# Third head in PSUM, two powers as one operation, GpSimd's additions side by side, and DVE's top keys in front of the turn of the expert weights

## The reference, cut to what matters

```
n1  = layernorm(x)
q, k, v = n1 @ Wq.T, n1 @ Wk.T, n1 @ Wv.T ; sq, sk = elu(q) + 1, elu(k) + 1
memory_part = (sq @ memory) / clip(sq @ memory_norm)
local_part  = causal linear attention(sq, sk, v), in chunks of 128, with a state S += sk.T @ v per chunk
x_mid = x + layernorm((g * memory_part + (1 - g) * local_part) @ Wo.T)

n2  = layernorm(x_mid)
dense   = silu(n2 @ Wup.T) @ Wdown.T                          # inner size 1024
routing: 4 heads, each with 64 + 64 key scores; top 8 of both sides, the 8 best of their sums
w       = silu((n2 . down_embed[i]) * softmax(best sums))     # for the 8 chosen of 1024 experts, per head
experts = sum of w * up_embed[i] over heads and choices
out = x_mid + layernorm(dense + experts)
```

## Time and profile before

| what | value |
|---|---|
| median of 3 runs | 2870.93 us (2860.86 to 2872.65) |
| profiled execution | 2865.48 us, its span 2863.7 us |
| PE (TensorE) busy | 2790.7 us, 97% |
| DVE busy | 2550.8 us, 89% |
| ACT (ScalarE) busy | 2547.9 us, 89% |
| POOL (GpSimd) busy | 2320.0 us, 81% |
| chain that ended last | POOL 50%, DVE 26%, issue 10%, PE 7%, ACT 5% |
| granted TensorE clock | 0.998 |

### The profile page before, as it was taken

The page is one execution under the profiler, slowest core; times in us unless marked ns, Lnnn a source line. Parts: engine busy times, 40 slices in busy tenths (PEclk is TensorE's granted clock), DMA queues, the critical chain, the costliest instruction groups (busy, mean ns, idle before and its releaser), DMA issues.

```text
span 2863.7 us, 46938 instructions
## 1 busy us (share of the span) xinstructions
PE 2790.7 (97%) x13306; PEld 2178.3 (76%) x13306; DVE 2550.8 (89%) x6346; ACT 2547.9 (89%) x3692; POOL 2320.0 (81%) x2556
## 2 busy tenths in 40 slices
PE   8999999999999999999999999999999999999998
PEld 7677777777777777777777777777777777777776
DVE  6898899999998899999999999999999899998886
ACT  6888988899889898998898989988999899899997
POOL 5767788788888888888888888888888888888884
PEclk9999999999999999999999999999999999999999
DMA  4787887788878887888788778877887788788764
GB/s 134 152 165 161 175 169 165 159 173 173 169 158 175 162 174 158 171 174 170 158 178 170 164 164 173 169 165 166 173 174 161 168 173 173 162 175 170 146 155 114
DMA packets 609031, 471.50 MB, mean 165 GB/s; under 512 B 362371, under 2 KB 543492, under 8 KB 608772
## 3 DMA queue, kind: packets, MB, share of 16 engines
q0 software_dynamic: 52832, 199.77, 39.5%
q1 hardware_dynamic: 555940, 268.74, 38.2%
HBM read 137.37 MB, written 131.20 MB: 94 GB/s over the span
## 4 chain that ended last, share of the span: by engine, by line
POOL 50%; DVE 26%; issue 10%; PE 7%; ACT 5%; DMA 0%; DVEq 0%; POOLq 0%; ACTq 0%
POOL sums L678 21%; POOL rstd L626 13%; PE banks L854 6%; POOL wexp L753 5%; DVE prob_odd L1426 4%; DVE w_blocks L1460 4%; POOL h_diff L657 3%; POOL cand_best L736 2%; DVE x_mid L1551 2%; POOL cdif L756 2%; DVE sums L1384 2%; ACT wexp L1152 2%; POOL hT L670 2%; ACT wexp L1155 2%; DVE picked L1388 2%
## 5 line engine op out<-in xcount | busy, mean ns | idle before, releaser
L678 POOL TENSOR_TENSOR sums<-scores 128x1024 f32<-128x1024 f32 x512 | 1022.2, 2111 | 70.4 <-ACT scores L1286 63.1
L626 POOL TENSOR_TENSOR rstd<-var_eps,minus_half 128x1 f32<-128x1 f32 x512 | 554.8, 1164 | 46.1 <-ACT y_sq L1141 21.0
L854 PE MATMUL banks<-deT,xn2T 128*128 128x512 f32 x1024 | 482.5, 594 | 2.6 <-DVE picked L1388 2.2
L854 PE MATMUL banks<-xn2T,wupT 128*128 128x256 f32 (+1 forms) x2272 | 465.4, 359 | 3.2 <-DVE state L1519 2.5
L854 PE MATMUL banks<-ue,gT 128*128 128x256 f32 x2048 | 464.5, 380 | 3.0 <-ACT gT L1216 3.0
L854 PEld LDWEIGHTS banks<-ue,gT 128*128 128x128 f32 x2048 | 390.0, 191 | 56.6 <-ACT gT L1216 3.4
L854 PEld LDWEIGHTS banks<-xn2T,wupT 128*128 128x128 f32 x2272 | 390.1, 191 | 46.5 <-DVE state L1519 3.3
L854 PEld LDWEIGHTS banks<-deT,xn2T 128*128 128x128 f32 x1024 | 185.3, 191 | 135.1 <-issue 124.4
L1152 ACT ACTIVATE wexp<-prob_odd 128x1024 f32<-128x1024 f32 x127 | 134.4, 1059 | 134.0 <-DVE w_blocks L1460 133.8
L854 PE MATMUL banks<-route,xn2T 128*128 128x512 f32 x512 | 240.8, 592 | 0.8 <-ACT xn2T L1116 0.8
L854 PE MATMUL banks<-wdownT,hT 128*128 128x128 f32 (+1 forms) x1608 | 239.3, 294 | 0.1
(11 more groups left out here) (190 smaller groups left out, 7272.7 us busy)
## 6 DMA issues: line engine op xcount, KB each, us to landing
wexp<-wexp POOLq DMA_DIRECT2D x127, 1024.0 KB, 10.4
wexp<-wexp POOLq DMA_DIRECT2D x127, 512.0 KB, 5.2
w_way<-w_blocks SPq DMA_DIRECT2D x127, 512.0 KB, 3.1
g_parts<-w_way SPq DMA_DIRECT2D x508, 128.0 KB, 7.6
xn_way<-xn_blocks SPq DMA_DIRECT2D x992, 32.0 KB, 1.7
x_in<-_attn_hidden_states_dram SPq DMA_DIRECT2D x128, 128.0 KB, 6.0
out_dram<-x_out SPq DMA_DIRECT2D x128, 128.0 KB, 4.6
xn1T<-xn_way SPq DMA_DIRECT2D x125, 128.0 KB, 3.9
```

Source lines behind the costliest of these rows:

```text
L626: return nc.gpsimd.tensor_tensor(rstd[:, n, m:m + 1], var_eps[:, n, m:m + 1], minus_half[:, :], ALU.pow)
L678: return nc.gpsimd.tensor_tensor(sums[:, k, :, :], scores[:, k, 0:XIN].unsqueeze(2).broadcast_to([P, XIN, NKEYS]), scores[:, HEADS + k, :] ...
L854: last = nc.tensor.matmul(out, lhs(c), rhs(c), start=(start and c == 0), stop=(stop and c == chunks - 1), skip_group_check=shared)
```

## The change

TOPS = TILES makes the first of two places for the top keys the only one: ahead of the turn L1460. GpSimd's body is put in another order, and two powers are one operation where a step has both. Head 2's pick is written over `down` in PSUM, in place of `picked[:, 0, :]`. TensorE then waits for head 2's weighing.

```diff
-    TOPS = 3
+    TOPS = TILES
...
+        def with_y(k):
+
+            found = [u for u in (k - 7, k - 6) if u >= 0 and seven(u) == (k - u == 7)]
+            return found[0] if len(found) == 1 else None
...
+            def two_powers(a, b):
+                cols = slice(a, b + 1, b - a)
+                r, v = (x[:, :, :].rearrange("p n m -> p (n m)")[:, cols] for x in (rstd, var_eps))
+                return nc.gpsimd.tensor_tensor(r, v, minus_half[:, :].broadcast_to([P, 2]), ALU.pow)
...
             def body(t, steady):
+                if t[7] is not None:
+                    pool.wait_ge(s_mix_var_eps, t[7] + 1)
+                    if with_y(t[7]) is None:
+                        power(LN_O, t[7] % 2).then_inc(s_mix_rstd, 1)
+                    else:
+                        pool.wait_ge(s_y_var_eps, with_y(t[7]) + 1)
+                        two_powers(2 * LN_O + t[7] % 2, 2 * LN_Y + with_y(t[7]) % 2).then_inc(s_mix_rstd, 1)
                 if t[9] is not None:
                     key_sums(3).then_inc(s_head_3_sums_ready, 1)
-                if t[7] is not None:
-                    pool.wait_ge(s_mix_var_eps, t[7] + 1)
-                    power(LN_O, t[7] % 2).then_inc(s_mix_rstd, 1)
...
+                for y in ([t[14]] if seven(t[14]) else []) + ([t[13]] if plain(t[13]) else []):
+                    if t[7] is None or with_y(t[7]) is None:
+                        pool.wait_ge(s_y_var_eps, y + 1)
+                        power(LN_Y, y % 2).then_inc(s_y_rstd, 1)
+                if t[7] is not None:
+                    pool.wait_ge(s_x_mid_var_eps, t[7] + 1)
+                    power(LN_M, t[7] % 2).then_inc(s_x_mid_rstd, 1)
                 if seven(t[11]) and t[11] % 2 == 0:
                     h_difference(t[11])
                 if seven(t[12]) and t[12] % 2 == 0:
                     h_three(t[12])
-                if seven(t[14]):
-                    pool.wait_ge(s_y_var_eps, t[14] + 1)
-                    power(LN_Y, t[14] % 2).then_inc(s_y_rstd, 1)
-                if plain(t[13]):
-                    pool.wait_ge(s_y_var_eps, t[13] + 1)
-                    power(LN_Y, t[13] % 2).then_inc(s_y_rstd, 1)
-                if t[7] is not None:
-                    pool.wait_ge(s_x_mid_var_eps, t[7] + 1)
-                    power(LN_M, t[7] % 2).then_inc(s_x_mid_rstd, 1)
...
                 if seven(t[11]):
-                    pool.wait_ge(s_head_3_weighed, t[9] + 1)
                     if t[11] % 2 == 0:
                         h_second_row(t[11])
...
                 if t[9] is not None:
                     if t[9] == 0:
                         pe.wait_ge(s_set_sb, SET_DOWN)
-                    if not steady:
-                        wait(pe, s_head_2_selected, t[9])
+                    wait(pe, s_head_2_weighed, t[9])
                     product(d_ps[0], DC, lambda c: xn2T[:, c, t[9] % TURNED, :], lambda c: deT[:, c, 0:HALF]).then_inc(s_down_0_in_psum, 1)
...
                     dve.wait_ge(s_head_2_sums_ready, t[10] + 1)
-                    dve.wait_ge(s_head_0_weighed, t[10] + 1)
-                    nc.vector.scalar_tensor_tensor(picked[:, 0, :], head(sums, 2), best[:, 2, TOP - 1:TOP], down,
+                    nc.vector.scalar_tensor_tensor(down, head(sums, 2), best[:, 2, TOP - 1:TOP], down,
                                                    ALU.is_ge, ALU.mult).then_inc(s_head_2_selected, 1)
...
-                    nc.vector.scalar_tensor_tensor(prob[2], picked[:, 0, :], rz[:, t[10] % 2, 2:3], prob[2],
+                    nc.vector.scalar_tensor_tensor(prob[2], down, rz[:, t[10] % 2, 2:3], prob[2],
                                                    ALU.mult, ALU.mult).then_inc(s_head_2_weighed, 1)
```

More of the change, by code:

```diff
@@ L403, in y_bank, with y_rstd_made @@
             return bank[{TILES - 3: 5, TILES - 2: 1, TILES - 1: 2}.get(t, 4)][:, first:first + D]
+        def with_y(k):
+            found = [u for u in (k - 7, k - 6) if u >= 0 and seven(u) == (k - u == 7)]
+            return found[0] if len(found) == 1 else None
+        def y_rstd_made(eng, t):
+            partners = [k for k in range(TILES) if with_y(k) == t]
+            if partners:
+                eng.wait_ge(s_mix_rstd, partners[0] + 1)
+            else:
+                eng.wait_ge(s_y_rstd, len([u for u in range(t + 1) if not [k for k in range(TILES) if with_y(k) == u]]))
         def y_made(eng, t):
@@ L1343, in x_made @@
                 wait(dve, s_x_stored, 16 * t)
-                dve.wait_ge(s_y_rstd, t + 1)
+                y_rstd_made(dve, t)
                 nc.vector.scalar_tensor_tensor(x_out[:, :], y_sb[:, t % 2, 0:D], rstd[:, LN_Y, t % 2:t % 2 + 1], x_mid[:, t % MID_SLOTS, :],
```

## The result

The changed kernel takes 3003.15 us (median of 4 runs, 3002.84 to 3003.61), the kernel before 2870.72 (4 runs, 2860.86 to 2872.65): a ratio of 1.046, 95% interval 1.0426 to 1.0491. It is slower, as forecast, but by 132 us and not by 70, and 3003 us lies above the range 2895 to 2985.

The account below looks back on a forecast made before the run. A ring of GpSimd and DVE bounds the kernel at 21.98 us a step; ScalarE's closed ring makes it 22.6. Over 107 steps 66 us, plus 4 at the end, on 2865.5, with 5.4 for the median: 2940 us, range 2895 to 2985.

Parts of the forecast that it names:

- The ring that the change closes: ScalarE's copy of the scores, DVE's tops and turn, then L1152: at least 2.54 us from copy to L1152.
- Step two: The step without `cross_added`: turn, ScalarE's mix copy, TensorE, relu, copy of the scores, tops, turn; 22.79, taken as 22.8 us.
- Step one: The step with `cross_added`: ScalarE's own work 22.09 us, the ring through DVE 22.33; taken as 22.4 us.
- Two powers as one: On GpSimd: a power of two columns takes 0.6 us, between 0.55 and 1.10; gain nothing.
- Power for `x_mid` ahead of the sums: On GpSimd, ahead of head 3's sums: the 29.3 us of waits at `x_mid` go.
- Wait of the h additions removed: GpSimd no longer waits for head 3: 1.8 us earlier, then waits for the copy of the scores; worth nothing.
- Head 2 in PSUM: DVE's pick: one wait on itself less, about 0.1 us; bounded by -0.1 and +0.2, taken as 0.
- The first steps nothing, the last 4 us: Ends of the run: first steps add nothing, as tops went first there already; the last 14 add 0.3 us each.
- TensorE's idle time moves to the state's addition: Sign of being right: TensorE's idle time then lies behind ScalarE's mix copy.
- A: Rival, faster: the ring of GpSimd and DVE was the bound and nothing takes its place; 2830 us, chance 5%.
- B: Rival, the same: TensorE's part has slack, only ScalarE's own work counts; 2865 to 2880 us, chance 8%.
- C: Rival: GpSimd's h addition or head-3 sums obstruct DVE's L1532, `x_out` or L1426; 0.3 to 0.5 us a step, 2965 to 3010, 17%.

Follow-up runs that it names:

- T and P alone: The kernel before with the top keys ahead of the turn and head 2's pick in PSUM, GpSimd's order as before: 2952.86 us, ratio 1.028.
- P alone: The kernel before with only head 2's pick in PSUM and TensorE's wait for head 2's weighing: 2806.95 us, ratio 0.976.
- T alone: The kernel before with only the top keys ahead of the turn of the expert weights (TOPS = TILES): 2980.02 us, ratio 1.039.

## Why the prediction was right in its direction and wrong in its size

- *The ring that the change closes*: right. Copy, tops, turn, silu of head 3 bound the changed kernel; the gap was never below 2.61 us (forecast 2.5), and ScalarE's order alone gave 104 and 111 us back. The edit named as the one that costs takes 109 to 146 us, of which 20 to 30 us stay when ScalarE's order is changed.
- *Step two, 22.8*: right, 22.83.
- *Step one, 22.4*: this is the step that failed. "The sums hold until about 8.4 us (8.9 with a power of 1.10), and L1532 wants to start at 7.95 ... That is 0.2 to 0.75 us, step one 22.5 to 23.1" stands in the working, and then 22.4 was taken for the sum. The sums held until 8.92 us, the weighing took 0.68 us longer than with T and P alone, and step one was 23.06. 23.06 and 22.83 in place of 22.4 and 22.8 is 0.35 us a step and more, with the irregular steps 0.45 (23.05 against 22.6): 49 of the 68 us by which the spans differ more than was forecast. A collision that the traces date to a tenth of a microsecond was left to a rival, at 17%, where it belonged in the sum. The collision put in at its full size would still have given too little: the prediction's own upper end, with 23.1 and 22.8, has 104 us for the 107 steps and 8 for the ends, where 114.7 and 23.5 were measured. The Trainium skill's rule ("SBUF — State Buffer", "Who interferes with whom") gave the upper end for the right reason; this trace agrees, with 2.06 us for L1549.
- *Two powers as one, 0.6*: wrong. It took 1.07 us: nothing is saved by joining them, and the sums behind it end at 8.92 and not at 8.4 us. With 0.6 they would still have ended after the weighing's start at 7.95, so the joint power made the collision longer and did not make it.
- *Power for `x_mid` ahead of the sums*: the wait did go (29.3 to 1.1 us). It was no gain: with the sums back in front, the time fell by 28 us.
- *Wait of the h additions removed, "Worth nothing by itself"*: wrong. It cost 10 to 15 us here and 94 us on P alone. The wait kept a GpSimd operation of 1.3 us out of the stretch in which DVE works on SBUF.
- *Head 2 in PSUM, "about 0.1 us", "take 0"*: wrong. It gave 64 us by itself, 0.65 us of a typical step. In the changed kernel it is worth 124. The bound of -0.1 to +0.2 looked at L1388 alone, and not at who stands while L1406 runs; the earlier trace rows had the case in which DVE is the one that stands, and the 42.1 us of `xn`'s waits for a power were the other one. Even the power of 1.50 us in the earlier trace rows, which takes 0.55 when nothing holds it, was such a case: DVE's L1532 of the earlier trace rows runs beside it. The duration was right: 1.28 us to PSUM, and L1423, which reads it, 1269 ns.
- *The first steps nothing, the last 4 us*: too low, 9.4 and 14.1. T alone is already 7.6 us later at the turn of the earlier trace rows (200.20 against 192.57); "tops went first there already" holds for three tiles only.
- *TensorE's idle time moves to the state's addition*: it did (81.9 us new there), but the wait at the masked product stayed (47.8, 58.9).
- *Rivals*: A and B fell. C, much slower by obstruction, named what came on top of the ring and, with 2965 to 3010, the time; of the operations it named, the sums in front of head 1's weighing cost most, and the late h addition stood under `xn`, which it did not name.

## What to carry to other kernels

Before an operation that frees a tile another engine needs is put behind one that waits for that same engine, close the ring on paper: here one reordering without any new instruction cost 109 us and more. Where operations of DVE with two inputs in SBUF meet GpSimd's, write down both start times, put the collision into the sum and not among the risks, and count both directions: a GpSimd operation that stands under one of DVE can cost as much as the other way round. A wait that seems idle may be what keeps two engines apart; try its removal alone, as every part of a bundle: here the one good part, 2.4% by itself, was buried under two that cost more.

## What the runs showed of the hardware

- A power of two columns on GpSimd took 1.07 us, where one of one column took 0.55: twice the columns took twice the time, at these two sizes.
- `xn`, a one-input DVE operation of 128x256 in fp32 with its two scalars from columns, took 1.69 us beside a GpSimd addition and 0.40 without (1192 and 408 ns in the mean of two runs that differ in the wait alone). So not only operations with two SBUF inputs collide.
- It doesn't need a long GpSimd operation: two powers of one column took 2.17 us, in place of 1.06 to 1.09, beside a DVE operation of 1.28 us with two SBUF inputs.
- Small operations lose the most in proportion: a 128x112 mask on DVE went from 0.27 to 1.98 us behind 1024-column sums.
- DVE writing 1024 fp32 columns over its own input in PSUM took 1.28 us, as when it writes to SBUF.
